# Local attention in one pass: blocks of 64 queries against 128 keys, exponentials kept and transposed, and a written-out order of slices

## The reference, cut to what matters

```python
# per layer, 8 heads of 64, window 64, scores scaled by 8
bk, bv = (look_around(bk), look_around(bv))      # block w sees the keys of blocks w-1 and w
sim = jnp.einsum('bhwid,bhwjd->bhwij', bq, bk)   # 64 queries x 128 keys
mask = (i < j) | (i > j + WINDOW) | (j == -1)
sim = jnp.where(mask, -jnp.finfo(sim.dtype).max, sim)
attn = jax.nn.softmax(sim, axis=-1)
out = jnp.einsum('bhwij,bhwjd->bhwid', attn, bv)
```

## Time and profile before

| | before |
|---|---|
| median of 3 runs | 2546.24 us (2540.85 to 2549.43) |
| profiled execution | span 2549.1 us, which is what the page gives of its time |
| PE busy | 1889.6 us (74%) |
| DVE busy | 1351.0 us (53%) |
| ACT busy | 1388.6 us (54%) |
| POOL busy | 554.6 us (22%) |
| DMA | 76.26 MB, mean 30 GB/s |

### The profile page before, as it was taken

One profiled execution on the slowest core, in us unless ns is written; L12 is line 12 of the kernel. 1 busy time (PEld: TensorE's weight loads), 2 busy tenths in 40 slices (PEclk: granted clock), 3 DMA queues, 4 the chain that ended last, 5 costly groups with the idle time before them and its releaser, 6 DMA issues.

```text
span 2549.1 us, 53778 instructions
## 1 busy us (share of the span) xinstructions
PE 1889.6 (74%) x22054; PEld 1123.1 (44%) x22054; DVE 1351.0 (53%) x3132; ACT 1388.6 (54%) x3607; POOL 554.6 (22%) x613
## 2 busy tenths in 40 slices
PE   4138656887769777887779776877688776986877
PEld 3014333545444544445444444445354544454444
DVE  5133446555554737464654646364655565473553
ACT  1154535764476726764476537673576547662534
POOL 2710204030221105030412014020403022110330
PEclk9659867998789878998789888998889978997999
DMA  9203360002000110002000201002100201000000
GB/s 280 61 2 89 110 162 19 3 1 51 10 10 2 27 34 9 3 1 52 14 6 1 51 10 10 2 4 49 17 3 1 51 10 10 2 8 13 1 1 5
DMA packets 129890, 76.26 MB, mean 30 GB/s; under 512 B 76082, under 2 KB 121610, under 8 KB 127596
## 3 DMA queue, kind: packets, MB, share of 16 engines
q1 hardware_dynamic: 125548, 66.51, 10.8%
q0 software_dynamic: 4096, 6.32, 2.0%
HBM read 41.71 MB, written 33.16 MB: 29 GB/s over the span
## 4 chain that ended last, share of the span: by engine, by line
issue 35%; PE 27%; DVE 14%; ACT 10%; POOL 7%; another core or an unknown queue 3%; SPq 2%; DMA 1%; DVEq 0%; POOLq 0%; ACTq 0%
PE PS L1290 4%; PE PS L1431 4%; PE PS L594 3%; POOL area_b L1738 2%; DVE work_a L973 2%; ACT work_a L812 2%; PE PS L1442 2%; DVE area_b L1623 2%; PE PS L750 2%; PE PS L566 2%; PE PS L1323 1%; POOL area_b L1746 1%; PE PS L486 1%; ACT work_a L795 1%
## 5 line engine op out<-in xcount | busy, mean ns | idle before, releaser
L1738 POOL TENSOR_TENSOR area_b<-area_b,tables 128x256 f32<-128x256 f32 x256 | 213.1, 852 | 765.5 <-DVE area_b L1623 765.5
L795 ACT ACTIVATE work_a<-PS,work_a 128x512 bf16<-128x512 f32 (+3 forms) x512 | 265.2, 541 | 139.9 <-DVE work_a L922 116.5
L922 DVE TENSOR_REDUCE work_a<-PS 128x2 f32<-128x1024 f32 (+3 forms) x256 | 201.2, 820 | 157.2 <-PE PS L486 94.1
L486 PE MATMUL PS<-strip,pick 64*128 64x128 bf16 (+4 forms) x2560 | 251.8, 278 | 0.0
L1527 ACT ACTIVATE area_b<-PS,neg_max 128x192 f32<-128x192 f32 (+1 forms) x512 | 202.6, 423 | 78.1 <-DVE neg_max L1663 55.1
L812 ACT ACTIVATE work_a<-PS 128x1024 f32<-128x1024 f32 (+1 forms) x192 | 169.5, 883 | 111.3 <-PE PS L486 110.8
L1290 PE MATMUL PS<-wqkv,area_b 128*128 128x512 f32 x384 | 205.4, 668 | 9.4 <-DVE area_b L1623 9.0
L532 PE MATMUL PS<-work_a 64*128 64x512 bf16 (+3 forms) x512 | 78.9, 352 | 160.8 <-ACT work_a L795 125.4
L1323 PE MATMUL PS<-area_b 64*128 64x192 f32 (+1 forms) x1024 | 143.6, 410 | 69.5 <-ACT area_b L1527 57.3
L594 PE MATMUL PS<-work_a 128*64 128x512 f32 (+3 forms) x1024 | 187.2, 467 | 4.0 <-ACT work_a L812 4.0
L1752 POOL TENSOR_TENSOR rstd_b<-var_eps_b,minus_half 128x4 f32<-128x4 f32 x16 | 16.4, 1027 | 751.0 <-DVE var_eps_b L120 751.0
(11 more groups left out here) (310 smaller groups left out, 3894.6 us busy)
## 6 DMA issues: line engine op xcount, KB each, us to landing
work_a<-stack_d SPq DMA_DIRECT2D x32, 512.0 KB
stack_d<-area_b SPq DMA_DIRECT2D x48, 192.0 KB, 3.1
stack_d<-area_b SPq DMA_DIRECT2D x32, 128.0 KB, 2.5
area_b<-in_L_attn_x_dram SPq DMA_DIRECT2D x4, 512.0 KB, 6.4
slots_in<-work_a SPq DMA_DIRECT2D x8, 256.0 KB, 4.9
stack_d<-work_a SPq DMA_DIRECT2D x4, 512.0 KB, 7.2
work_a<-xnT_d SPq DMA_DIRECT2D x8, 256.0 KB
work_a<-in_L_attn_x_dram SPq DMA_DIRECT2D x8, 256.0 KB
```

The lines of the kernel that those rows point to most:

```text
L486: return nc.tensor.matmul(to, pick16[half_rows(e), half * P:(half + 1) * P], rows, start=False, stop=True, tile_position=(64 * e, 0), skip ...
L795: nc.scalar.activation(dump0[:, n % 2 * T:n % 2 * T + (i + 1) * P], PS[:, a:a + (i + 1) * P], ACT.Exp, bias=neg_max0[:, k:k + 1], accum_ou ...
L922: nc.vector.reduce_max(neg_max0[:, 2 * g * NT + i:(2 * g + 2) * NT:NT], at[:, :, Q_AT[i]:Q_AT[i] + (i + 1) * P], AX_X, negate=True).then_i ...
L1738: nc.gpsimd.tensor_tensor(to[:, n, :, r, :], src[:, n, :, 1 - r, :], table(2 * n + 1, t)[:, 32 * r:32 * r + 32].unsqueeze(1).to_broadcast( ...
```

## The change

Part 1, local attention. The two passes become one. There are now 8 units, one for each pair of heads `g` and each `d` of 0 and 1. A unit holds all 512 queries of two half-heads: in the partitions 64c to 64c+63 stand the queries of the odd or even blocks of 64 (block w = 2i + c) of head `e = c ^ d`. Each block of 64 queries meets its 128 keys (64 for the first), so a unit fills one bank (4 or 5) with 128 x 512 scores. Masks come from two matmuls of 512 columns and one of 64 (`edges`). DVE takes one maximum per unit. ACT writes exponentials, which are now kept, with their sums. DVE takes reciprocals of the sums and multiplies. PE transposes four tiles of 128 x 128, ACT copies them to `probsT2`, and PE multiplies with the values. The keys of a block begin 64 rows before it, so odd blocks use `v2` and even blocks `v2_back`, a copy of the values shifted by 64 rows that two DMAs write, issued from ACT's queue. Logs, shift parts, `select16` and the second scoring are gone. The loop has 11 steps of two slices each.

```diff
-            for m in range(8):
...
-                        nc.tensor.matmul(PS[:, a:a + n], q2[half_rows(e), g * T + i * P:g * T + (i + 1) * P],
...
+            def scores(u):
+                g, d = divmod(u, 2)
+                if u >= 2:
+                    pe.wait_ge(s["sum"], past("sum", 4 * (u - 1)))
+                for i in range(NT):
+                    for c in range(2):
+                        e, w = c ^ d, 2 * i + c
+                        n = P if w else WIN
+                        a = (4 + d) * BANK + P * (i + 1) - n
+                        nc.tensor.matmul(PS[half_rows(c), a:a + n],
+                                         q2[half_rows(e), g * T + w * WIN:g * T + (w + 1) * WIN],
+                                         k2[half_rows(e), g * T + (w + 1) * WIN - n:g * T + (w + 1) * WIN],
+                                         start=(i == 0), stop=False, tile_position=(64 * e, 64 * c),
+                                         skip_group_check=True)
+                for c in range(2):
+                    edges(c ^ d, c, bank(4 + d)[half_rows(c), :].rearrange("p (i j) -> p i j", i=NT), 2, 2, NT)
+                edges(d, 0, bank(4 + d)[half_rows(0), 0:WIN], 1, 1).then_inc(s["scores"], 1)
+
+            def turn_probs(u):
+                pe.wait_ge(s["probs"], past("probs", u + 1))
...
+                for n in range(4):
+                    last = nc.tensor.transpose(bank(6, n * P, (n + 1) * P),
+                                               unit2(probs2, u, 3)[:, n * P:(n + 1) * P], ident)
+                last.then_inc(s["probs_T"], 1)
+
+            def context(u):
+                g, d = divmod(u, 2)
+                pe.wait_ge(s["probsT_copied"], past("probsT_copied", u + 1))
...
+                for i in range(NT):
+                    for c in range(2):
+                        e = c ^ d
+                        v = (i * H2 + 2 * g + e) * D2
+                        a = i * P + c * WIN
+                        last = nc.tensor.matmul(PS[half_rows(e), 7 * BANK + a:7 * BANK + a + WIN],
+                                                (v2_back, v2)[c][:, v:v + D2], unit2(probsT2, u, 2)[:, a:a + WIN],
+                                                start=True, stop=True, tile_position=(0, 64 * e),
+                                                skip_group_check=True)
+                last.then_inc(s["context"], 1)
+
+            for m in range(UNITS2 + 3):
+                if m < UNITS2:
+                    fill(2)
+                    scores(m)
+                yield
+                if m >= 3:
+                    context(m - 3)
+                if 2 <= m < UNITS2 + 2:
+                    fill(1)
+                    turn_probs(m - 2)
                 yield
```

The same loop on ACT and DVE:

```diff
+            act.wait_ge(s["v_copied"], past("v_copied", NT))
+            act.dma_start(v2_back[0:64, 512:], v2[64:P, 0:3 * 512]).then_inc(s["v_back"], 16)
+            act.dma_start(v2_back[64:P, :], v2[0:64, :]).then_inc(s["v_back"], 16)
...
+                for i in range(NT):
+                    a = (4 + u % 2) * BANK + P * i
+                    nc.scalar.activation(unit2(probs2, u, 3)[:, i * P:(i + 1) * P], PS[:, a:a + P], ACT.Exp,
...
+                nc.scalar.copy(unit2(probsT2, u, 2), bank(6)).then_inc(s["probsT_copied"], 1)
...
+            def maxima(u):
+                dve.wait_ge(s["scores"], past("scores", u + 1))
+                nc.vector.reduce_max(neg_max2[:, 4 * u:4 * u + 4], bank(4 + u % 2).rearrange("p (i c) -> p i c", c=P),
...
+                nc.vector.reciprocal(inv_sums2[:, 4 * u:4 * u + 4], sums2[:, 4 * u:4 * u + 4]).then_inc(s["inv_sum"], 1)
...
+                nc.vector.tensor_tensor(part, part, inv_sums2[:, 4 * u:4 * u + 4].unsqueeze(2).to_broadcast([P, 4, P]),
+                                        ALU.mult).then_inc(s["probs"], 1)
```

Part 3, the order. The counts are replaced by a written list of runs for the whole program, one string per engine, and a layer of B has 39 slices instead of 34:

```diff
-                order += ["A"] * (ahead - order.count("A")) + ["H"]
...
+            return [stream for run in ORDER[engine].split() for stream in run[0] * int(run[1:])]
```

More of the change, by code:

```diff
@@ L40 @@
 G2 = H2 // 2
-HH = H2 // 2
-KX = P + WIN
+UNITS2 = 2 * G2
 QK = 2 * H2 * D2
@@ L1302, in local_pe @@
                 yield
-            def shifts_T(half, k):
-                pe.wait_ge(s["shift_parts"], past("shift_parts", 3 * half + 3))
-                for i in range(NT):
-                    a = (half * NT + i) * P
-                    last = nc.tensor.transpose(bank(k, i * P, (i + 1) * P), shift_parts2[:, a:a + P], ident)
-                last.then_inc(s["shiftT"], 1)
             pe.wait_ge(s["turned_q"], past("turned_q", NT))
@@ new lines, in probsT_copied @@
+            def probsT_copied(u):
+                act.wait_ge(s["probs_T"], past("probs_T", u + 1))
+                if u >= 2:
+                    act.wait_ge(s["context"], past("context", u - 1))
+                nc.scalar.copy(unit2(probsT2, u, 2), bank(6)).then_inc(s["probsT_copied"], 1)
+            for m in range(UNITS2 + 3):
+                if m < UNITS2:
+                    exponentials(m)
+                yield
+                if 1 <= m <= UNITS2:
+                    probsT_copied(m - 1)
@@ L1680, in local_dve @@
+            for m in range(UNITS2 + 3):
+                if m < UNITS2:
+                    maxima(m)
+                yield
+                if 1 <= m <= UNITS2:
+                    probabilities(m - 1)
+                if m >= 4 and m % 2 == 0:
+                    g = (m - 4) // 2
+                    dve.wait_ge(s["context"], past("context", 2 * g + 2))
+                    nc.vector.tensor_copy(ctx2T[:, g * T:(g + 1) * T], bank(7)).then_inc(s["ctxT"], 1)
                 yield
@@ L1748, in local_pool @@
                 yield
-            for n in range(8 + 9 + 1):
+            for n in range(2 * (UNITS2 + 3) + 1):
                 yield
@@ L2282, in network @@
+        ORDER = {
+            "tensor":
[18 rows of a table added]
+            "scalar":
[16 rows of a table added]
+            "vector":
[15 rows of a table added]
+            "gpsimd":
[3 rows of a table added]
+            "sync":
+                "H11 A4 H1 A3 H1 A32 H5 A1 H1 A3 H2 A6 H1 A1 H1 A1 H4 A1 H2 A5 H3 A1 H2 A4 H7 A13 H1 A1 H1 A4 H1 A6 H1 A7 "
+                "B77 A93 B78 A93 B78 A93 B78 A93 B78 A93 B78 A93 B78 A93 B79 ",
         }
         def slices(engine):
-            total = B * (A_SLICES + D_SLICES)
-            if len(A_AHEAD_OF_HEAD[engine]) != H_SLICES or len(A_AHEAD_OF_B[engine]) != DEPTH * B_SLICES:
-                raise ValueError("one count per slice of the head, and of stream B")
@@ L2289, in slices @@
-            order = []
-            for ahead in A_AHEAD_OF_HEAD[engine]:
-                order += ["A"] * (ahead - order.count("A")) + ["H"]
-            for b in range(B):
-                for ahead in A_AHEAD_OF_B[engine]:
-                    order += ["A"] * (min(ahead + b * (A_SLICES + D_SLICES), total) - order.count("A")) + ["B"]
-            return order
+            return [stream for run in ORDER[engine].split() for stream in run[0] * int(run[1:])]
         with nc.Block() as block:
```

286 lines of the change are left out of this document (62 added, 224 removed), and 52 rows, old and new, of the table ORDER.

## The result

The changed kernel takes 2446.27 us (median of 4 runs, 2441.23 to 2450.62), the kernel before 2547.84 in the runs beside it. The ratio is 0.961, with a 95% interval of 0.959 to 0.964. The prediction said 2448. The total was right; the terms under it were right only in part, the agreement within 2 us is partly luck, and the experiments show where.

The account below looks back on a forecast made before the run. No engine is full, so waits between engines and the two streams sharing them set the time. From 2549.1 us, 84 for the mix and 14 for the tail were taken: 2451, or 2448 as median; range 2360 to 2555.

Parts of the forecast that it names:

- PE, per layer: Local attention on PE: eight new steps of 2.7 to 3.2 us replace 25.6 us; gain 4.0 us or none, taken 2.
- Pairs queue: Rival (d), score and mask matmuls: partners sharing a bank run in turn, 11.6 us more PE per layer; 2576 us, chance 0.05.
- ACT, per layer: Local attention on ACT: 20.4 us of work become 15.6 to 17.6 us, 3 to 5 us less.
- DVE: Local attention on DVE: 12.2 us of work become 15.2 us, 3 us more, hidden behind PE.
- Copy of the values: Two DMAs before the first context matmul: expected in time, costed at nothing; if late, up to 7.2 us per layer.
- Table loads at nothing: ACT's table loads move but stay as many, 117 before and 116 after, so they were costed at nothing.
- The gather at nothing: POOL's gather moved ahead of layer 0's rotary products: gain and loss cancel, bounds -5 to +5 us a batch.
- Tail -14: Local attention alone in the tail: 30 us against 37, 7 us less per layer, 14 for two layers.
- Mix, 4.9 us a step: Local attention beside stream A: 11 steps, 54 us, about 6 us less per layer, 84 over 14 layers.
- rival (a): The relay fades: steps in the mix take 4.5 us or less, 10 us less per layer; 2386 us, chance 0.24.
- (c): Loop of 11 steps: pieces of A stand between all six handovers; 6.0 us a step gives 2624 us, chance 0.13.
- (b): Mixed stretches do not shrink since stream A's chain is as long; only the tail gains, 2532 us, chance 0.10.

Follow-up runs that it names:

- e5: The new kernel without the three fillers in each step of the last batch's local attention: 2445.8 us, ratio 0.962.
- e4: The new kernel with the two inner loops of the score matmuls exchanged, so that partners no longer follow each other: 2478.8 us, ratio 0.976.
- e8: The kernel before with only the helper that remembers ACT's table set added: 2520.0 us, ratio 0.989.
- e12: The new kernel with layer 0's first gelu moved behind one slice of stream A on ACT, in seven batches: 2446.2 us, ratio 0.961.
- e3: The new kernel with POOL's queue alone in the old order, the gather again behind layer 0's rotary products: 2562.8 us, ratio 1.007.
- e1: The new kernel's code with the old order stretched over its slices, ACT and DVE aligned to PE by a crude rule in the local attention: 2583.3 us, ratio 1.017.
- e11: The kernel before with only DVE and ACT aligned to PE by a crude rule in the local attention: 2717.8 us, ratio 1.070.
- e9: The new kernel in its own order, DVE and ACT aligned to PE by a crude rule in seven batches' local attention: 2594.1 us, ratio 1.019.

## Why the prediction was right, point by point

- **PE, per layer.** Taken -2 us, bounds 0 and -4. Reckoned as in the prediction, the last stretch has 24.5 us less 23 fillers of 7.7 us together, 16.8, against 25.6; in e5, with the fillers out, it has 19.8. So -6 to -9 us, outside my bounds. The step is 3.04 us with three fillers, and the rest of it takes 2.3: scores 0.82 us for four pairs (I had 1.12), transposes 0.44 (0.66), context 0.62 (0.58 to 1.12), masks 0.42 (0.33). I had priced the transposes by their duration, and the scores by a pair that stands alone between other matmuls (0.28 us), where four in a row take 0.21 each.
- **Pairs queue.** Refuted by the timeline above. The Trainium skill's rule (TensorEngine Tiling (Array Packing), "Restrictions and Gotchas") that different row tiles cannot access one PSUM bank at once does not show here: partners that write the two halves of rows of one bank start 0.01 us apart, and e4 prices their concurrency at 0.4 us a step. But my reason for going against the rule was a misreading. In the code of L712 the bank goes by the row group (`BANK * c`), and what shares a bank are the four column groups of one row group. So the earlier trace rows says nothing of row groups in one bank, and the low chance of (d) came out right by luck.
- **ACT, per layer.** 16.1 us against 20.4 before: -4.2, or -3.1 with its two DMA issues, which busy time leaves out and the prediction had in its sum: within the -3 to -5. The issues take 0.47 and 0.61 us, and lie in the wait for the first maximum.
- **DVE.** +1.4 us a layer, not +3, and hidden as forecast: its total rose by 29 us, not 50.
- **Copy of the values.** It landed in 3.7 and 5.6 us; no wait for it is listed. Nothing, as taken.
- **Table loads at nothing.** Right as a count, not shown as a price: 29 go by the helper and 28 come back elsewhere. The 29 were worth 23 us in e8, and 14 of the 28 nothing in e12; what the other 14 cost was not run.
- **The gather at nothing.** This step failed as worked out. I weighed 2 to 3 us of delay against the 5.06 us of the earlier trace rows. The rotary products do start 7.1 us after the first `qkv` matmul instead of 5.7, but in e3, without the early gather, they start after 6.9 (batch 3), so the gather delays them by no more than 0.3 us; and the wait is gone. But I had costed "the rest of the order" apart from it, at nothing. It is one move: the first pieces of A go up into the projections (11 slices instead of 7 on PE), and that only works with the rows there. Undone by itself it costs 16 us a period.
- **Tail -14.** The two attentions gave 8.8 us each, not 7; the projections before them took back some 3 us, 15 in all. There is no stream A here to be placed, so the order has no part in it, and e1 has the shorter tail too.
- **Mix, 4.9 us a step.** The steps are 42.8 / 11 = 3.9 us in layer 0 and 51.1 / 11 = 4.6 in layer 1, both near rival (a), while the period is that of the forecast. The step that failed is the assumption that A's share of the stretch stays: 22 and 18 slices became 17 and 15. What the code gives under equal shares is e1 against e11, 9 us a layer in the attention, table loads included; I had 6. There is also a slip in the sum: 59.4 less my 54 us is 5.4, which I rounded to 6; unrounded, the mix would have given 76 us and the forecast 2456.
- **Slower by the long step, (c).** It decides from 5.4 us per step. In e1 a step takes 5.3 us in layer 0 and 6.2 in layer 1, and e1 is slower than before. So the time of (c) does come with an order that does not fit. But its mechanism, that a long step suffers more from the pieces of A, isn't shown: the same placing costs the short steps of the kernel before 174 us (e11) and the long ones 148 (e9).
- **Stream A sets the period, (b).** Refuted: periods fell by 12.4 us.
- **Why the total agrees.** The 84 us of the mix came out as 87, but not from the terms that the sum gave it. It had 12 us a period for the code and nothing for loads and order. The controls give the code 8 to 11 us, and where the pieces stand is worth over 100 us in e3, e9 and e11. That the written list of the new kernel brings nearly what was forecast for the code alone is luck.

## What to carry to other kernels

When two streams are interleaved by hand, price the change and the order together, and when you split them in an experiment, run a control with the same crude order on the old code: e1 alone would have given the wrong verdict. Equal counts (here of table loads) between two kernels do not show that nothing happened; look where they stand, and count them in the controls too. Before moving a DMA issue, list who needs its data in the new order, not only whom it delays.

## What had not been expected of the hardware

An operation of DVE on 128 x 128 numbers takes 1.28 us in the new kernel while POOL runs an addition of its own, and 0.29 us in e3, where POOL is idle. The new kernel:

```profile
1234.54 1.59 POOL L1695 TENSOR_TENSOR area_b<-area_b 128x512 f32<-128x512 f32 x1
1234.93 1.28 DVE L911 TENSOR_SCALAR work_a<-work_a 128x128 f32<-128x128 f32 x1
```

and e3:

```profile
1284.27 0.29 DVE L911 TENSOR_SCALAR work_a<-work_a 128x128 f32<-128x128 f32 x1 [17.83 <-DMA work_a<-slots_out,work_a]
1284.66 0.61 POOL L1121 TENSOR_SCALAR work_a<-work_a 128x128 f32<-128x128 f32 x1 [4.56 <-DVE work_a L911]
```

All seven batches show it (median 1280 ns against 286). DVE's operation ends at 1236.21, just behind POOL's at 1236.13: it looks as if DVE waited inside its instruction until POOL was done. The Trainium skill (SBUF — State Buffer, "SBUF: two separate sides") says that DVE and GpSimd share a pair of ports as an exclusive lock, that a DVE operation in a 2-port mode or with two inputs in SBUF takes part in it, and that the later one fully blocks; by that rule, the trace agrees: POOL's addition starts first. Which mode DVE's operation runs in no row shows, and the rule was not tested by itself. What made DVE stand for 5.06 us beside the gather in the kernel before stays open too: in the new kernel DVE works from 1203.9 on while the gather is issued until 1209.4, and its wait just before (5.97 us, for ACT) is there in e3 too, without the gather (6.85 us).
